# Grouped attention: rows of probabilities are normalised by a product with a diagonal matrix instead of being multiplied by the pool engine and then transposed

## The reference, cut to what matters

```python
B, SQ, HIDDEN = (2, 256, 256)            # the input here is 1 x 1024 x 256
HEADS, GROUPS, KVC = (16, 4, 128)
q = jnp.einsum('bsh,he->bse', x, w_q).reshape(b, sq, GROUPS, HPG, KVC)
kv = jnp.einsum('bsh,he->bse', x, w_kv)
k, v = jnp.split(kv, 2, axis=-1)
scores = jnp.einsum('bqgpd,bkgd->bgqpk', q, k) * (SCALE / LAYER_INDEX)
scores = jnp.where(causal[None, None, :, None, :], scores, -jnp.inf)
probs = jax.nn.softmax(scores, axis=-1).astype(x.dtype)
ctx = jnp.einsum('bgqpk,bkgd->bqgpd', probs, v).reshape(b, sq, HEADS * KVC)
return jnp.einsum('bse,eh->bsh', ctx, w_dense)
```

## Time and profile before

| | |
|---|---|
| median of 3 runs | 1169.88 us (1167.11, 1169.88, 1632.95) |
| profiled execution | 1164.86 us, span 1162.9 us |
| TensorE busy | 993.2 us (85%) |
| vector engine busy | 777.1 us (67%) |
| ACT busy | 584.7 us (50%) |
| POOL busy | 401.2 us (35%) |
| grouped attention loop | about 678 to 1087 us of the span |

### The profile page before, as it was taken

One profiled execution on the slowest core, in us unless ns is written; L12 is line 12 of the kernel. 1 busy time (PEld: TensorE's weight loads), 2 busy tenths in 40 slices (PEclk: granted clock), 3 DMA queues, 4 the chain that ended last, 5 costly groups with the idle time before them and its releaser, 6 DMA issues.

```text
span 1162.9 us, 20943 instructions
## 1 busy us (share of the span) xinstructions
PE 993.2 (85%) x7768; PEld 663.2 (57%) x7768; DVE 777.1 (67%) x1923; ACT 584.7 (50%) x1172; POOL 401.2 (35%) x261
## 2 busy tenths in 40 slices
PE   1799769888888888889989978889898989888697
PEld 1477612333333333478867746666666667666586
DVE  6846887787888785154587656666766666666654
ACT  1634224656665666643365445454545555455264
POOL 4010140224413440000035045454545455455344
PEclk8799857999999999989989999999999999999999
DMA  7010345315532411022000000000000000000001
GB/s 172 1 73 3 112 116 88 61 48 84 92 61 57 79 30 65 2 73 73 1 37 0 1 1 1 1 2 1 2 1 1 1 1 1 1 2 1 1 1 36
DMA packets 25685, 40.25 MB, mean 35 GB/s; under 512 B 3104, under 2 KB 21152, under 8 KB 23808
## 3 DMA queue, kind: packets, MB, share of 16 engines
q1 hardware_dynamic: 25584, 38.93, 14.3%
HBM read 32.88 MB, written 5.84 MB: 33 GB/s over the span
## 4 chain that ended last, share of the span: by engine, by line
PE 33%; DVE 10%; issue 4%; ACT 3%; POOL 0%; DVEq 0%; POOLq 0%; ACTq 0%
PE bank L1032 12%; PE pair L1367 7%; PE bank L1408 6%; DVE mx L1741 4%; PE bank L1396 4%; PE bank L1124 2%; DVE PT L1774 2%; ACT QH L792 1%; DVE xn L1756 1%; DVE xn L1506 1%; PE bank L1060 1%; ACT PT L792 1%; DVE stats L1496 0%; DVE rec L1766 0%; PE pair L1369 0%
## 5 line engine op out<-in xcount | busy, mean ns | idle before, releaser
L784 POOL TENSOR_SCALAR P<-P,rec 128x1024 f32<-128x1024 f32 (+7 forms) x128 | 220.5, 1724 | 213.4 <-DVE rec L1766 213.3
L908 ACT ACTIVATE PT<-bank 128x512 f32<-128x512 f32 (+2 forms) x320 | 159.6, 554 | 95.5 <-PE bank L1211 67.8
L1637 DVE CUSTOM_DVE_ANT_0 bank<-bank,stripS 128x512 f32<-128x512 f32 (+3 forms) x256 | 147.9, 606 | 31.9 <-PE bank L1184 30.4
L1184 PE MATMUL bank<-KT,QT 96*128 96x512 bf16 (+3 forms) x384 | 124.6, 362 | 32.9 <-DVE MX L1637 21.0
L1396 PE MATMUL bank<-ident,P 128*128 128x128 f32 x576 | 99.1, 281 | 45.9 <-DVE PT L1774 33.7
L1367 PE MATMUL pair<-KH,QH 128*128 128x512 f16 (+3 forms) x576 | 115.4, 328 | 5.6 <-ACT P L974 4.2
L974 ACT ACTIVATE P<-pair,nm 128x1024 f32<-128x1024 f32 (+7 forms) x128 | 95.5, 746 | 43.8 <-DVE nm L1745 43.8
L1408 PE MATMUL bank<-PT,VH 128*128 128x128 f16 x1728 | 117.3, 219 | 0.1
L1195 PE MATMUL bank<-QT,KT 128*128 128x512 bf16 (+3 forms) x384 | 103.0, 333 | 11.1 <-ACT PT L908 8.9
L1408 PEld LDWEIGHTS bank<-PT,VH 128*128 128x128 f16 x1728 | 107.0, 98 | 2.8 <-DVE PT L1774 0.2
L792 ACT ACTIVATE PT<-bank 128x384 f16<-128x384 f32 (+1 forms) x192 | 88.1, 489 | 39.9 <-PE bank L1396 39.1
(11 more groups left out here) (178 smaller groups left out, 1956.5 us busy)
## 6 DMA issues: line engine op xcount, KB each, us to landing
stripS<-band_rows SPq DMA_DIRECT2D x32, 128.0 KB, 2.2
KT<-qk_dram SPq DMA_DIRECT2D x21, 192.0 KB
qk_dram<-parts SPq DMA_DIRECT2D x12, 256.0 KB, 2.2
cprow<-cp SPq DMA_DIRECT2D x9, 256.0 KB, 11.1
stripT<-seq_dram SPq DMA_DIRECT2D x24, 88.0 KB, 9.2
q_raw<-w_gu SPq DMA_DIRECT2D x4, 512.0 KB, 10.7
w_raw<-w_dense SPq DMA_DIRECT2D x2, 1024.0 KB, 6.7
w_raw<-w_q SPq DMA_DIRECT2D x2, 1024.0 KB, 4.9
```

What stands on the lines that cost most here:

```text
L784: pool.tensor_scalar(rows, rows, rec1[:, m % 4:m % 4 + 1], None, ALU.mult).then_inc(s["pn"], 1)
L908: act.activation(PT[:, jb % 2, h0 + hs[0]:h0 + hs[-1] + 1, o:o + ni], src, ACT.Exp).then_inc(s["s2_exp"], 1)
L1184: pe.matmul(ring_bank(use)[:, 0:nj], queries(g)[0:ROWS, h, P * ib:P * (ib + 1)], KT3[0:ROWS, g % 3, h, j0:j0 + nj], start=True, stop=True) ...
L1637: dve.tensor_tensor_reduce(out, out, stripS[:, h, HALF - nj:HALF], 1.0, LOWEST, ALU.add, ALU.max, mx).then_inc(s["s1_max"], 1)
```

## The change

The pool engine no longer multiplies the rows. It multiplies the 128x128 identity by the 128 reciprocals, one for each row, and so writes a diagonal matrix into one of four new buffers `diag1`. TensorE no longer turns a piece by a transposition with the identity. It makes an ordinary 32-bit product of the same piece of `P1`, as the loaded operand, with the diagonal matrix as the moving one: that turns the piece and scales it. A diagonal may be overwritten once the tiles of the step four before have been made (a wait of POOL on `tp`). The rest of the diff gives the bank of a use a name (`rt_bank`) and changes nothing else.

```diff
@@ -288,6 +288,7 @@
         P1 = z("P1", [P, 3, S], F32)
+        diag1 = z("diag1", [P, 4, P], F32)
         PT1 = z("PT1", [P, 3, 2, S], F16)
...
+
+        def rt_bank(use):
+            return bank[4 + at_rt[use] % 2]
...
             for m in range(STEPS):
                 pool.wait_ge(s["rec_"], m + 1)
-                rows = P1[:, m % 3, 0:P * (block_of(m) + 1)]
-                pool.tensor_scalar(rows, rows, rec1[:, m % 4:m % 4 + 1], None, ALU.mult).then_inc(s["pn"], 1)
+                if m >= 4:
+                    pool.wait_ge(s["tp"], count_rt(("t", m - 4, tiles_t(m - 4)[-1])))
+                pool.tensor_scalar(diag1[:, m % 4, :], ident, rec1[:, m % 4:m % 4 + 1], None, ALU.mult).then_inc(s["pn"], 1)
...
                             for b in range(min(4, block_of(m) + 1 - 4 * c)):
-                                ins = pe.transpose(bank[4 + at_rt[use] % 2][:, P * b:P * (b + 1)], P1[:, m % 3, HALF * c + P * b:HALF * c + P * (b + 1)], ident)
+                                ins = pe.matmul(rt_bank(use)[:, P * b:P * (b + 1)], P1[:, m % 3, HALF * c + P * b:HALF * c + P * (b + 1)], diag1[:, m % 4, :],
+                                                start=True, stop=True, skip_group_check=True)
                             ins.then_inc(s["tp"], 1)
```

More of the change, by code:

```diff
@@ L952, in queries_high @@
                 act.wait_ge(s["qp"], 2 * h + c + 1)
-                copy(QH1[:, h % 2, 0, HALF * c:HALF * (c + 1)], bank[4 + at_rt[("q", h, c)] % 2]).then_inc(s["qp_hi"], 1)
+                copy(QH1[:, h % 2, 0, HALF * c:HALF * (c + 1)], rt_bank(("q", h, c))).then_inc(s["qp_hi"], 1)
             def grouped():
@@ L992, in grouped @@
                             nb = min(4, block_of(m) + 1 - 4 * c)
-                            copy(PT1[:, m % 3, 0, HALF * c:HALF * c + P * nb], bank[4 + at_rt[use] % 2][:, 0:P * nb]).then_inc(s["tp_hi"], 1)
+                            copy(PT1[:, m % 3, 0, HALF * c:HALF * c + P * nb], rt_bank(use)[:, 0:P * nb]).then_inc(s["tp_hi"], 1)
                     if 0 <= n < STEPS:
@@ L1323, in make_q @@
                 wait_rt_bank(pe, use)
-                products(bank[4 + at_rt[use] % 2], lambda p, k: WQ1[:, p, k, DH * h:DH * (h + 1)],
+                products(rt_bank(use), lambda p, k: WQ1[:, p, k, DH * h:DH * (h + 1)],
                          lambda p, k: ln(p, k, HALF * c, HALF), PASSES3).then_inc(s["qp"], 1)
@@ L1376, in dense @@
                     wait_rt_bank(pe, use)
-                    products(bank[4 + at_rt[use] % 2], lambda p, k: WO1[:, p, 2 * b + k, P * (c % 2):P * (c % 2 + 1)],
+                    products(rt_bank(use), lambda p, k: WO1[:, p, 2 * b + k, P * (c % 2):P * (c % 2 + 1)],
                              lambda p, k: CT1[k][:, p, HALF * (c // 2):HALF * (c // 2 + 1)], PASSES3).then_inc(s["dn"], 1)
@@ L1716, in queries_low @@
                 cols = slice(HALF * c, HALF * (c + 1))
-                dve.tensor_tensor(QH1[:, h % 2, 1, cols], bank[4 + at_rt[("q", h, c)] % 2], QH1[:, h % 2, 0, cols], ALU.subtract).then_inc(s["qp_lo"], 1)
+                dve.tensor_tensor(QH1[:, h % 2, 1, cols], rt_bank(("q", h, c)), QH1[:, h % 2, 0, cols], ALU.subtract).then_inc(s["qp_lo"], 1)
             def grouped():
@@ L1750, in accumulate @@
                     acc = ACC1[:, c % 2, HALF * (c // 2):HALF * (c // 2 + 1)]
-                    src = bank[4 + at_rt[use] % 2]
+                    src = rt_bank(use)
                     if b == 0:
@@ L1773, in grouped @@
                             cols = slice(HALF * c, HALF * c + P * nb)
-                            dve.tensor_tensor(PT1[:, m % 3, 1, cols], bank[4 + at_rt[use] % 2][:, 0:P * nb], PT1[:, m % 3, 0, cols], ALU.subtract).then_inc(s["tp_lo"], 1)
+                            dve.tensor_tensor(PT1[:, m % 3, 1, cols], rt_bank(use)[:, 0:P * nb], PT1[:, m % 3, 0, cols], ALU.subtract).then_inc(s["tp_lo"], 1)
                     if n >= 0:
```

## The result

The changed kernel takes 1202.62 us (median of 4 runs, 1201.70 to 1204.06) where the kernel before takes 1169.88 (median of its three fast runs, 1167.11 to 1171.92; a fourth, slow one of 1632.95 is not counted). The ratio is 1.0283 with a 95% interval of 1.0253 to 1.0313: **slower by 2.8%, 33 us**. The forecast was 1202 with a range of 1178 to 1238.

The account below looks back on a forecast made before the run. TensorE, not full, was taken to bound the loop. 32.2 us for pieces on the path plus 2.2 for first loads, on the profiled 1164.86 us, gave 1199.3; 3 more made 1202 us, range 1178 to 1238.

Parts of the forecast that it names:

- What bounds the loop: Grouped loop: TensorE, busy 361 of 409 us, idles 45.9 us ahead of transpositions, mostly released by vector engine bank reads.
- POOL: POOL's multiplications in the grouped loop: the 143 us saved were to be worth nothing on the path.
- POOL's new wait: POOL's wait for tiles four steps back, before overwriting a diagonal: claimed long over, nothing taken for it.
- The price of a piece: Each turned piece on TensorE: two records of 0.115 us, 0.230 in all, 0.121 us more than a transposition.
- What lies on the path: Pieces on the loop's chain cost in full, others hide in waits: 4.02 us per two heads, 32.2 for 16.
- the first loads: First load of a tile may stand open, 0.051 us in eleven places a period: 2.2 us taken, 4.5 at most.
- the 31 pieces: Pieces of the 72 in two heads that stand on the chain that ended last: 3.75 us added per period.
- All swallowed: Rival: TensorE's waits and tails swallow all the added work they can hold: +8 us, 1176 us; chance 0.13.
- nothing covered: Rival: no wait on TensorE hides any of the added work: +69.7 us, 1238 us; chance 0.14.
- Open loads: Rival: each TensorE record lasts as long as its 0.191 us load: +95 us, about 1263 us; chance 0.06, shared.
- the single record: Rival: the ordinary product stays one record, so nothing changes on TensorE: 1168 us; chance 0.04.
- the faster case: Rival: POOL's multiplication is on the path, so waits at second tiles go, up to 45.9 us: about 1122; chance 0.03.

Follow-up runs that it names:

- between_before: Kernel before, with the values products of blocks 4 to 7 issued on TensorE between the first and second turned tile: 1141.87 us, ratio 0.9732.
- pool_alone: Changed kernel with the transposition kept: POOL makes the diagonals, unused, and leaves the rows unnormalised: 1169.28 us, ratio 0.9995 to the kernel before.
- product_alone: Kernel before, with every piece turned by an ordinary 32-bit product with the identity; POOL still multiplies the rows: 1203.13 us, ratio 1.0281.
- first_of_two: Kernel before, with only the first tiles of blocks 4 to 7 (256 of 576 pieces) turned by ordinary products with the identity: 1172.50 us, ratio 1.0021.
- all_others: Kernel before, with second tiles of blocks 4 to 7 and tiles of blocks 0 to 3 turned by ordinary products with the identity: 1197.06 us, ratio 1.0228.
- twice: Changed kernel with each diagonal product made twice into the same place: 1304.99 us, ratio 1.1154 to the kernel before.

## Why the prediction was right

- **What bounds the loop.** Right: TensorE, with waits for two shared banks. `between_before` shows that the waits were free room: 30 us less idle, about 30 us less time.
- **POOL.** Right that it is worth nothing: `pool_alone` 0.9995. I had this from one interval of 1.5 us and a wait of 0.2 us. I wrote that POOL's new wait is long over, while the profile puts 52.4 us of POOL's idle time, at 16 places, down to TensorE's tiles. The trace settles it for what I wrote: at all 16 places POOL starts 0.09 to 0.10 us after the end of the vector engine's reciprocal, as it does at the other 112 (0.08 to 0.11). So it waited for the reciprocal, and the tiles are only the releaser that the profile inferred. `product_alone`, without that wait, takes the same time.
- **The price of a piece.** Two records, as read off the row sums: 1152, with loads of 191 ns. A record takes 0.111 us, not my 0.115. So a piece costs 0.113 more, not 0.121. That the record was bounded from a form with one moving column and one with 32 loaded columns did no harm, since both bounds were within 0.02 us.
- **What lies on the path.** Right in kind: `first_of_two` (+0.2%) and `all_others` (+2.3%) show that the place of a piece decides and not the number of pieces. The sum for a period was 4.02 us, 4.30 with the first loads, and it measured 4.04. Two errors partly cancel in it. The pieces were priced too high: with 0.113 the 31 pieces give 3.50 and the odd head's second tile of block 7 another 0.20, together 3.70 instead of 4.02. The first loads were priced too low: 0.34 is left for them, where I had 0.28. That this rest is theirs is read from the two chains and no run isolates it. The tile of four pieces takes 1.16 us on the chain where it took 0.66, the next 0.94 for 0.55, the next 0.50 for 0.22. That is 0.50, 0.39 and 0.28 more, where four, three and two pieces make 0.45, 0.34 and 0.23. So each of these tiles carries 0.05 us beyond its pieces, as much as its load is longer (191 ns against 140). The longest record of the product lasts 377 ns against a median of 275, the longest transposition 333 against 273, which is the same 0.05.
- **The rivals.** All swallowed (1176) and nothing covered (1238) both lose, and `twice` shows why they lie on either side: there were about 58 us of room in all, which is what the first one says, but the first 65 us of work could reach only 32 of them. Open loads fall with the spacing of 0.111, the single record with the 1152 records, and the faster case with `pool_alone`.
- **The signs in the new profile.** Idle time under 20 us: 13.8. The vector engine still the releaser: yes. POOL 77 us: 77.5. The clock at 1.00: yes. The loop some 34 us longer: 32.3 from the first to the last turned piece.
- **That 1202 was hit to the microsecond** is luck. The forecast was 34.4 us on top of a base of 1167.9 (the profiled execution of the kernel before plus the 3 us that I added). Measured were 32.7 us on top of 1169.88. The rise was 1.7 us too large and the base 2.0 too low, and the two errors cancel.

## What to carry to other kernels

Price a longer instruction at two rates: in full where it stands on the chain that ended last, and at nothing where it stands in front of a wait that is longer, the previous product's tail included; then put the sum against one period of the loop. A wait that swallows an addition is also room that can be filled: moving independent products into it was worth 2.7% here and needed no new buffer. Before an eviction is moved ahead of other work in an engine's queue, look at who waits for that other work; here the exponential did, and it cost 5%. A long wait named in the trace (POOL, 36 us) is no gain until it is taken away, for another wait may stand right behind it.

## What the runs showed of the hardware that I had not expected

- An ordinary 32-bit product of a 128x128 piece with 128 columns is two loads and two records, 0.111 us apart, 0.222 in all, and the transposition of the same piece is one of 0.109. The loads of 191 ns are hidden, although they are longer than the records' spacing, all but some 0.05 us at the head of a tile. The Trainium skill, TensorE: Matmul & The Clock Gate, section Terms, gives the transpose mode as 4 times faster for FP32; the runs show a factor of 2.
- The same product in the rounded 32-bit type is one record of about 0.11 us also with only 128 moving columns.
- The granted clock fell to 1.2 GHz for 3.4 us in six places of the loop with rounded products and did not with transpositions or two-record products, though the transpositions have the same 46 us of idle time ahead of the tiles. These places lie behind the loop's entry; at the entry, about 680 us, it fell once in most of the runs. In one of these places TensorE had idled 1.14 us at the second tile of block 7, which the kernel before does too (1.15 us) without a fall. The falls are not bound to the rounded type: in the order with the low parts first, where TensorE waits more, they came with transpositions as well (five and eight), and not with the two-record product. With the waits filled there was no fall behind the entry with any kind of product. Why rounded products and transpositions differ at the same idle time is open.
